# A vision tower's last attention batch and its routing: who adds the output bias, and when the low parts of the experts' matrices are made

## The reference, cut to what matters

```python
h = ssm_tokens(x)                                   # (8, 256, 512)
h = concat([cls_tok, h], axis=1)                    # 8 class rows, 257 rows a batch
h = h + attention(layernorm(h))                     # 16 heads, 512 wide
y = layernorm(h)
logits = y @ router_w + router_b                    # 8 experts
gates  = softmax over the two largest, 0 elsewhere
expert_out = gelu(y @ expert_w[e] + expert_b[e])    # 8 matrices of 512 x 512
h = h + (sum of gates * expert_out) @ out_w + out_b
```

## Time and profile before

| what | us |
|---|---|
| median of three runs | 741.95 |
| the profiled execution's own time | 743.96 |
| its span | 742.2 |
| TensorE busy | 677.8 |
| VectorE busy | 525.4 |
| ScalarE busy | 412.8 |
| GpSimd busy | 152.6 |

### The profile page before, as it was taken

How to read it: one execution, slowest core, us unless ns; L and a number is a source line. 1 busy time by engine, 2 the same in 40 slices (tenths; PEclk the granted TensorE clock), 3 DMA queues, 4 the chain that set the end, 5 groups by cost and what they waited for, 6 DMA issues and landing times.

```text
span 742.2 us, 16679 instructions
## 1 busy us (share of the span) xinstructions
PE 677.8 (91%) x5671; PEld 541.1 (73%) x5672; DVE 525.4 (71%) x1210; ACT 412.8 (56%) x1073; POOL 152.6 (21%) x306
## 2 busy tenths in 40 slices
PE   4788977889999999999999999889679999998998
PEld 3577867767778787777878777656347888886886
DVE  7999883655788777787877877677884444445775
ACT  5864544486767677676766666665723333333111
POOL 5200001010121111201112020113132223336650
PEclk9889999979999999999999999999789999999999
DMA  7501255300000010000100003216626765556895
GB/s 202 198 1 29 115 143 145 73 1 1 3 29 30 0 56 0 29 28 14 42 0 28 28 28 115 85 58 227 256 60 207 206 202 162 167 168 204 263 325 172
DMA packets 54553, 76.11 MB, mean 103 GB/s; under 512 B 24666, under 2 KB 26970, under 8 KB 54387
## 3 DMA queue, kind: packets, MB, share of 16 engines
q1 hardware_dynamic: 40850, 42.43, 17.7%
q0 software_dynamic: 5920, 19.40, 9.9%
q10 hardware_dynamic: 7744, 13.77, 5.0%
HBM read 45.42 MB, written 30.16 MB: 102 GB/s over the span
## 4 chain that ended last, share of the span: by engine, by line
PE 72%; DVE 17%; ACT 4%; issue 3%; DMA 2%; POOL 1%; ACTq 0%; DVEq 0%; POOLq 0%; SPq 0%
PE ps L1978 45%; PE ps L2084 8%; PE ps L2094 4%; PE ps L2077 4%; PE ps L2145 3%; DVE ring L1409 3%; DVE ring L1408 3%; PE ps L1925 2%; PE ps L2101 1%; ACT prb L1029 1%; PE ps L1956 1%; ACT pts L1037 1%; DVE ew_lo L1720 1%; PE ps L1969 1%; PE ps L2044 1%
## 5 line engine op out<-in xcount | busy, mean ns | idle before, releaser
L1037 ACT ACTIVATE pts<-ps 128x512 f32<-128x512 f32 x128 | 77.0, 602 | 98.2 <-PE ps L2084 98.1
L1029 ACT ACTIVATE prb<-ps,negmax 128x257 f32<-128x257 f32 x256 | 117.7, 478 | 5.2 <-DVE negmax L1479 4.3
L1479 DVE TENSOR_REDUCE negmax<-ps 128x2 f32<-128x514 f32 x128 | 82.5, 686 | 22.4 <-PE ps L2077 22.4
L2084 PE MATMUL ps<-ident,prb 128*128 128x128 f32 x512 | 84.0, 287 | 5.7 <-ACT pts L1037 3.2
L2084 PEld LDWEIGHTS ps<-ident,prb 128*128 128x128 f32 x512 | 57.1, 143 | 30.8 <-issue 13.1
L1488 DVE TENSOR_SCALAR prb<-prb,rrec 128x258 f32<-128x258 f32 x256 | 73.5, 351 | 2.3
L1211 ACT ACTIVATE rows<-ps 128x512 f32<-128x512 f32 x40 | 23.9, 598 | 87.5 <-DVE ps L1835 85.5
L1978 PE MATMUL ps<-ew_hi,xnT_hi 128*128 x160 | 66.7, 417 | 3.0 <-DVE xnT_lo L1756 2.4
L1978 PE MATMUL ps<-ew_lo,xnT_hi 128*128 x160 | 63.5, 397 | 0.0
L1978 PE MATMUL ps<-ew_hi,xnT_lo 128*128 x160 | 63.0, 394 | 0.0
L839 POOL DMA_INDIRECT rows<-xn_dram,token_of x40 | 39.6, 990 | 106.9 <-PE ps L2145 87.1
(11 more groups left out here) (402 smaller groups left out, 1761.1 us busy)
## 6 DMA issues: line engine op xcount, KB each, us to landing
y_slots<-rows ACTq DMA_DIRECT2D x40, 256.0 KB
ew<-in_L_ffn_expert_w_dram SPq DMA_DIRECT2D x8, 1024.0 KB, 9.1
h_dram<-h_ob SPq DMA_DIRECT2D x17, 256.0 KB, 2.0
xn_dram<-tok SPq DMA_DIRECT2D x17, 256.0 KB, 2.2
h_late<-h_dram SPq DMA_DIRECT2D x12, 256.0 KB
out_dram<-h_late SPq DMA_DIRECT2D x11, 256.0 KB
y_slots<-u_sb SPq DMA_DIRECT2D x9, 256.0 KB, 5.4
tok_dram<-so SPq DMA_DIRECT2D x4, 512.0 KB, 3.1
```

Of the source, the lines that this page charges most:

```text
L1029: e = act.activation(prb[:, u % 2, j, 0:KEYS], ps[:, j, 0:KEYS], ACT.Exp, bias=negmax[:, u % 2, j:j + 1], accum_out=rowsum[:, u % 2, j:j + 1])
L1037: act.activation(pts[:, slot:slot + 2, :, st * P:(st + 1) * P], ps[:, 4, :].rearrange("p (h t s) -> p h t s", h=2, t=HALVES), ACT.Copy).th ...
L1479: dve.tensor_reduce(negmax[:, u % 2, 2 * b:2 * b + 2], ps[:, 2 * b:2 * b + 2, 0:KEYS], AX_X, ALU.max, negate=True).then_inc(s["dve_max"], 1)
L2084: mm = pe.transpose(ps[:, 4, (2 * j + tt) * P:(2 * j + tt + 1) * P], prb[:, u % 2, 2 * b + j, tt * P:(tt + 1) * P], ident[:, :])
```

## The change

It has three parts.

1. GpSimd no longer adds the output bias for the last batch's two tiles and the class tile; VectorE does, by `out_bias`, at the places where it made the low part of experts 0 and 1.
2. The first expert's high part is made by ScalarE in unit 3 of the last batch, its low part by VectorE in units 4 and 5, ahead of the statistics. The second expert's low part is made in halves: one after the norm of the last batch's tiles, one between two groups' logits.
3. After the routing, the gates' three instructions stand ahead of the wait for the slots' tokens. The three for `stores_used` and the low part of expert 5 stand behind `lo_xs(0)` and `lo_xs(1)`.

Two places in SBUF move with it: 280 words a partition ahead of `q_hi`, and `reached` ahead of `gates`.

```diff
 # GpSimd, after the last batch
-            for st in range(HALVES):
-                pool.wait_ge(s["dve_residual"], 2 * last + st + 1)
-                pool.wait_ge(st_h[st], 16 * NB)
-                add_bias(last, st)
             norm_pow(last)
             pool.wait_ge(s["dve_stats2"], 5 * NB + 3)
             pool.tensor_tensor(rsc[:, 1, :], rsc[:, 0, :], mhalf[:, :], ALU.pow)...
-            pool.wait_ge(st_h[0], 16 * (NB + 1))
-            pool.tensor_tensor(h_ob[:, 0, :], tok[:, CLS, :], ob[:, :], ALU.add)...
 # ScalarE, last batch and after
                     if u == 3 and last:
                         keep_xnT(1)
+                        act.wait_ge(s["pe_values"], NB * HALVES)
+                        hi_expert(0)
...
             hi_ot(last, 3)
-            hi_expert(0)
             hi_expert(1)
 # VectorE, after_norm
+                    if u == 4 and last:
+                        lo_chunks(0, 0, KC // 2)
+                    if u == 5 and last:
+                        lo_chunks(0, KC // 2, KC).then_inc(s["dve_expert_low"], 1)
...
                     if not first:
                         residual_stats(c - 1, u - 4)
 # VectorE, after the last batch
+            def out_bias(st, t):
+                dve.wait_ge(st_h[st], 16 * NB if t != CLS else 16 * (NB + 1))
+                dve.tensor_tensor(h_ob[:, st, :], tok[:, t, :], ob[:, :], ALU.add)...
             residual_stats(last, 0)
-            lo_chunks(0, 0, KC // 2)
+            out_bias(0, last)
             residual(last, 1, 7)
             residual_stats(last, 1)
             norm_sums(last)
-            lo_chunks(0, KC // 2, KC).then_inc(s["dve_expert_low"], 1)
+            out_bias(1, NB + last)
             for st in range(HALVES):
                 normalise(last, st)
+            lo_chunks(1, 0, KC // 2)
...
-            lo_expert(1)
+            out_bias(0, CLS)
             dve.wait_ge(s["pool_rstd"], NB + 1)
             # the class tile's norm
             for q in range(EARLY_QUADS + 1, len(QUADS)):
                 take_logits(q - 1)
                 top_two(q - 1)
+                if q == EARLY_QUADS + 1:
+                    lo_chunks(1, KC // 2, KC).then_inc(s["dve_expert_low"], 1)
 # VectorE, after the routing
+            # the gates' three instructions
             dve.wait_ge(s["pe_token_of"], 1)
             # token_of, slot_of, the experts' numbers
-            # the three instructions for stores_used
-            # the gates' three instructions
             lo_expert(2)
             lo_chunks(LOWS_IN_ATTENTION + 1, KC // 2, KC)
-            lo_chunks(LOWS_IN_ATTENTION + 2, 0, KC)
             lo_xs(0, 0)
             lo_xs(1, 1)
+            # the three instructions for stores_used
+            lo_chunks(LOWS_IN_ATTENTION + 2, 0, KC)
             lo_expert(LOWS_IN_ATTENTION + 3, 4)
```

More of the change, by code:

```diff
@@ L222, in vit_tower_kernel @@
         xhat = sb(at, "xhat", [P, HALVES, D])
+        sb(at, "rest_of_first_high", [P, 280])
         q_hi = sb(at, "q_hi", [P, KC, KPAD], F32R)
@@ L284, in vit_tower_kernel @@
         eb = sb(ffn, "eb", [P, NE, D])
+        reached = sb(ffn, "reached", [P, SLOTS, NE - 1])
         gates = sb(ffn, "gates", [P, NT, SEL])
@@ L331, in vit_tower_kernel @@
             "pool_rstd": "the second norm's 1 / sqrt for a batch",
-            "pool_out_bias": "a tile with the output bias added, to be kept for the end",
+            "out_bias_added": "a tile with the output bias added, to be kept for the end",
             "pool_sums_cleared": "zeros ahead of the tiles' sums, then where the running sums of an expert begin",
@@ L804, in add_bias @@
             def add_bias(m, st):
-                pool.tensor_tensor(h_ob[:, st, :], tok[:, st * NB + m, :], ob[:, :], ALU.add).then_inc(s["pool_out_bias"], 1)
+                pool.tensor_tensor(h_ob[:, st, :], tok[:, st * NB + m, :], ob[:, :], ALU.add).then_inc(s["out_bias_added"], 1)
             def norm_pow(m):
@@ L826, in _ @@
             pool.tensor_tensor(rsc[:, 1, :], rsc[:, 0, :], mhalf[:, :], ALU.pow).then_inc(s["pool_rstd"], 1)
-            pool.wait_ge(st_h[0], 16 * (NB + 1))
-            pool.tensor_tensor(h_ob[:, 0, :], tok[:, CLS, :], ob[:, :], ALU.add).then_inc(s["pool_out_bias"], 1)
             pool.memset(tiles_to[:, :, 0:4], 0.0).then_inc(s["pool_sums_cleared"], 1)
@@ L1067, in keep_lgT, with hi_expert @@
                 act.activation(dst[:, 0:w], ps[:, bank, 0:w], ACT.Copy).then_inc(s["act_logitsT_kept"], 1)
+            def hi_expert(e):
+                act.wait_ge(ld_ew[e], ew_from[e] + 16)
+                act.activation(ew_hi[:, e, :, :], ew[:, e, :, :], ACT.Copy).then_inc(s["act_expert_high"], 1)
             def body(c, first, last):
@@ L1561, in top_two, with lo_chunks, lo_expert @@
                 then(e)
+            def lo_chunks(e, k0, k1):
+                dve.wait_ge(s["act_expert_high"], e + 1)
+                return dve.tensor_tensor(ew_lo[:, e, k0:k1, :], ew[:, e, k0:k1, :], ew_hi[:, e, k0:k1, :].bitcast(F32),
+                                         ALU.subtract)
+            def lo_expert(e, done=1):
+                lo_chunks(e, 0, KC).then_inc(s["dve_expert_low"], done)
             def before_norm(c, u, first, last):
@@ L1717, in _ @@
                               ).then_inc(s["dve_spread"], 1)
[L1718 to L1724, removed]
+            def out_bias(st, t):
+                dve.wait_ge(st_h[st], 16 * NB if t != CLS else 16 * (NB + 1))
+                dve.tensor_tensor(h_ob[:, st, :], tok[:, t, :], ob[:, :], ALU.add).then_inc(s["out_bias_added"], 1)
             top_two(1)
@@ L1804, in _ @@
                                   bc(slot_place[:, c0:c1].unsqueeze(2), shape), ALU.is_equal).then_inc(s["dve_onehot"], 1)
+            dve.wait_ge(s["act_route_exp"], 1)
+            then(dve.tensor_scalar(spread[:, 2, :], spread[:, 1, :], 1.0, None, ALU.add))
+            then(dve.reciprocal(gates[:, :, 0], spread[:, 2, :]))
+            dve.tensor_tensor(gates[:, :, 1], gates[:, :, 0], spread[:, 1, :], ALU.mult).then_inc(s["dve_gates"], 1)
             dve.wait_ge(s["pe_token_of"], 1)
@@ L1839, in _ @@
             lo_xs(1, 1)
+            then(dve.tensor_scalar(pairs_used[:, 0:1], tiles_to[:, 1, 3 + NE:4 + NE], 0.5, 0.25, ALU.mult, ALU.add))
+            then(dve.tensor_scalar(pairs_used[:, 1:2], pairs_used[:, 0:1], ROUND_MAGIC, ROUND_MAGIC, ALU.add, ALU.subtract))
+            dve.tensor_scalar(stores_used[:, :], pairs_used[:, 1:2], 16.0, None, ALU.mult).then_inc(s["dve_stores_used"], 1)
+            lo_chunks(LOWS_IN_ATTENTION + 2, 0, KC)
             dve.wait_ge(s["act_w_low"], 5 * KC + 2)
```

12 lines of the change are left out of this document (4 added, 8 removed).

## The result

The changed kernel took 746.84 us, the median of 12 runs (743.41 to 750.68), beside 741.65 us for the kernel before (12 runs, 737.0 to 745.4). The ratio is 1.0071, with a 95% interval of 1.0052 to 1.0089: slower, by about 5 us. The forecast was 744.4, with 740.0 to 747.2 as its range; the measured time lies in it, 0.4 us from its upper end, and beyond the 0.5% up to which I spoke of no change; to slower by more than that I had given 0.24.

The account below looks back on a forecast made before the run. The chain was taken as 72% TensorE and 17% VectorE, with the change touching 90 us where it changes hands. Terms +1.2 - 1.7 + 2.15 + 0.8 = +2.45 us on the median 741.95 gave 744.4, range 740.0 to 747.2.

Parts of the forecast that it names:

- unit 5's half, no cover: Last batch, unit 5: half of expert 0's low part delays the statistics with no idle time to cover it, +1.2 us.
- clock in the last batch: TensorE's gap of 2.1 us in the last batch: clock falls earlier (0) or twice (+1.5); nothing was taken.
- bias and low parts, to the class logits: After the last batch: bias on VectorE and moved low parts, -1.7 us (bounds -1.0 and -1.9).
- the rest of the routing: From the class logits to the routing's end: a VectorE chain with nothing changed in it, 0.
- loop's first product after `token_of`: Experts' start: the loop's first product waits for VectorE's low parts and the late second fetch, +2.15 us.
- clock in the loop's first tile: TensorE stands before the loop, whose first tile may run slowly: 0 to +1.5 us, +0.8 taken.
- The cover in unit 4: Last batch, unit 4: 1.21 us of low part fits into 1.32 us of idle time before the maxima, by a tenth.
- The power that waits for VectorE's two-input instruction: After the last batch: GpSimd's power stands until a VectorE instruction with two SBUF inputs is over; first ends 0.6 us earlier.
- The class tile's turn, bound by TensorE: After the last batch: the turn moves from 521.52 to about 519.7, 1.85 us earlier, with no idle time before it.
- The second fetch: Experts' start: it stands until a boundary between VectorE's subtractions, taking 2.4 us in place of 0.96.
- first tile decides: Rival: TensorE bounds the experts' start from tile 0 on, the loop's first product 2.2 us earlier; 739.3 us, chance 0.09.
- the clock falls in all new gaps: Rival: TensorE's clock falls in the last batch's gap and before the loop, +1.5 us each; 746.6 us, chance 0.20.

Follow-up runs that it names:

- interleaved: Changed kernel with expert 0's half low part in unit 7 and low parts after the routing interleaved with the first splits: 737.55 us, ratio 0.9932.
- part3_undone: Changed kernel with the order after the routing put back as before: 744.78 us, ratio 1.0014.
- interleaved_half_in_u5: Changed kernel with the order of interleaved after the routing, but expert 0's half low part left in unit 5: 743.19 us, ratio 1.0008.
- fetch_between: Changed kernel with expert 2's low part made in four instructions of 512 elements instead of one of 2048: 745.52 us, ratio 1.0040.
- gap_filled: Changed kernel with eight never-read TensorE products in the gap before pv in unit 6: 743.25 us, ratio 1.0001.
- order_alone: Kernel before with only VectorE's order after token_of as in interleaved, without parts 1 and 2: 741.02 us, ratio 0.9989.
- interleaved_again: The same kernel as interleaved, measured again in another session: 740.07 us, ratio 0.9970 to the kernel before.

## Why the prediction was right or wrong

| step | predicted | profile |
|---|---|---|
| unit 5's half, no cover | +1.2 | +1.12 |
| clock in the last batch | 0 (up to +1.5) | +2.27 (A: 3.39 - 1.12) |
| bias and low parts, to the class logits | -1.7 | -1.88 |
| the rest of the routing | 0 | +0.31 |
| loop's first product after `token_of` | +2.15 | +1.81 (18.72, before 16.91) |
| clock in the loop's first tile | +0.8 (0 to +1.5) | +1.46 (E: 3.27 - 1.81) |
| sum | +2.45 | +5.09 |

The spans differ by 4.6, with the 0.66 from ahead of the change: 3.94 of the 5.09 arrive at the end. Before, the turns of the seventh and the sixth tile of slots are 4.05 us apart, after it 3.21; that is 0.8 of the 1.15 given back. That the measured time fell into the range at all is owed to its upper end, which took in two thirds of the case with the clock in full; the forecast of 2.45 had half of what the trace shows.

**The step that failed** is in the paragraph on TensorE's clock: "0 to +1.5 ... nothing for the first". I saw that the gap in unit 5 would be 2.1 us, and took it that a fall would only come earlier instead of later. It came earlier and stayed: 12.5 us at 0.59 in place of 4 us at 0.57. What that costs is in the table of A. A has two levels with the half elsewhere, 36.25 to 36.28 (six profiles) and 37.71 to 37.73 (before, interleaved), and two with it in unit 5, 37.38 to 37.40 and 41.12 to 41.16 (high: the changed kernel, part3_undone, interleaved_half_in_u5; low: fetch_between and gap_filled). So a fall costs 1.45 us without the wait in unit 5 and 3.75 with it. In each of the three high profiles with it the clock fell within a microsecond after `pv` of unit 6 began and was low for most of 12.5 us; in the two without it it fell one unit later and was low for most of 4. It is the length of the slow stretch that costs, not longer waits in it: TensorE's wait before the next `pv` is 0.75 us at the lower clock and 1.21 at the full one (gap_filled), since TensorE itself is late. Why a fall after this gap lasts longer, and why it comes in some executions only, no run shows. The bound of +1.5 was taken from the cost of one fall before, where it ended after 4 us; what a longer one costs no row showed. That the profile of before was itself one with a fall (37.73; order_alone, the same up to there, has 36.28) one execution could not tell.

**The steps that held.** The cover in unit 4 (0.17 us left of 1.32, a tenth predicted). The power that waits for VectorE's two-input instruction. The class tile's turn, bound by TensorE. The second fetch: predicted to take 2.4 us, measured 2.30, and shortened to 1.31 by more boundaries. The Trainium skill's page "SBUF — State Buffer", section "Who interferes with whom", infers that a `tensor_tensor` does not starve descriptor generation; for these fetches, which read their row numbers from SBUF, the measurements decide the other way, at least for the start of a fetch. It held too that tile 0's earlier start would be worth nothing, because the loop's first tile hangs on VectorE being through with all low parts: the "first tile decides" rival fell, with the first product 0.7 us earlier against `token_of` (8.17, before 8.90) and the loop's 1.8 later. The first split gained 2.1 us (5.89 after `token_of`, before 7.96), but TensorE had to turn the second tile first, whose rows came late; I had put the first product's gain at 2.2 without that.

**A size that was off**: +2.15 at the loop was 1.81, since the low parts' three instructions took 6.68 and not 6.8, and the second tile was turned 6.98 us after `token_of`, 0.3 earlier than I had reckoned.

**A term that was missing**: +0.31 in the routing, TensorE's last product of places, 0.85 us long at the lower clock, 0.53 before. It is a matter of the execution as well: C is 15.85 in interleaved and 15.55 in interleaved_again, one and the same kernel.

The rival "the clock falls in all new gaps" put the time at 746.6; measured were 746.84. So near a hit is partly luck: it too had only +1.5 for the batch, and its 4.65 stand beside 5.09 in the trace, of which 3.94 reached the end. I gave it 0.20 and the forecast 0.43. Against it I had set that the gap before 521.52 is as long, as if no fall had followed, and that two falls don't tell when the third comes. The trace of before says otherwise:

```profile
523.00:533.00 10.00, 7.01 (x21) 3.97 (x22) 8.29 (x37) 7.71 (x7) 0.00 (x0) 0.50 0.99 366
```

The clock was at the lower level from within 1.5 us after that gap, for 10 us, and once more from 540 to 543: four falls between 495 and 554, not two. That the gap brought it about is not shown, since the changed kernel has no gap there and yet a clock of 0.50 from 527 to 533.5; but it was no argument against the rival.

## What to carry to other kernels

Before an instruction is moved into a busy engine's queue, read the idle time that stands before the next instruction on that engine: the same 1.22 us were free in front of 1.32 us of idle time and cost about 3 us one unit later, in front of none. When TensorE gets a new gap, price it as the gap and a fall of the clock, with a chance for the fall and a range for how long it lasts; a single earlier fall gives neither. One profile of each kernel can then differ by more than the change does, so look at the mean clock of all runs too. When work is taken out from ahead of a first split, ask what the engine will do instead: if it then waits, the work has only moved to where more hangs on it; pieces between the splits keep both.

## What was not expected of the hardware

- A stretch at the lower clock has no fixed price. In the last batch it cost 1.45 us, or 3.75 us where the wait of TensorE ahead of it was 2.0 us and not 0.86, and profiles of the same instructions fall on one side or the other. The mean granted clock over the runs follows: 0.965 for the changed kernel, 0.971 with the half in unit 7.
- Eight products nobody reads, 2.08 us of TensorE's time in a gap, took the ratio to the kernel before from 1.0071 (1.0052 to 1.0089) to 1.0001 (0.9980 to 1.0021).
- A fetch by indirect DMA that meets a running subtraction of VectorE starts at its end or at the next boundary between two of them: 2.30 us with one of 2048 elements, 1.31 with pieces of 512, 0.94 alone. In the kernel before the fourth fetch, issued 1.1 us before such a subtraction ended, took 1.90.
- A good part of the scatter between executions is there before the change begins: unit 2's reciprocal lay between 466.72 and 471.27 us in 13 profiles of kernels whose instructions are the same up to there, while the 12 runs of the kernel before lay between 737.0 and 745.4.
